# A recurrence over pairs of tokens: scans of half the length, with the decay folded into k and r

## The chip, the cores and the metric

The kernel runs on one core of one Trainium2 chip. The metric is the device time of one execution in microseconds. The kernel before takes 1902.09 us (median of 3 runs, 1901.77 to 1902.61). In what follows PE is the matmul engine (PEld its weight loads), DVE the vector engine, ACT the scalar engine, POOL the general engine (GpSimd) and SP the engine that issues most DMAs.

## The reference

The input is 32 batches of 128 rows (channels) by 512. Two layers follow one another in each batch. The first is a cross attention between x and a context: both are normalised over their 512 columns, projected with 128x128 weights (Mn, Mm), multiplied to 512x512 scores, put through a softmax, and applied to a third projection; the input is added. The second layer is an RWKV block over 128 tokens of 512 features, with the context's first rows as its state. Its heart is a recurrence in 32 heads of 16x16 states:

```
xm = xa[:, :, None] + sx[:, :, None] * (maa_stack + xxx)        # five mixes of token t and t-1
w = exp(-exp(time_decay + tanh(xw @ td_w1) @ td_w2));  r, k, v = projections of their mixes
def step(s, rkvw):
    a = k_t[..., :, None] * v_t[..., None, :]
    out = einsum('bhi,bhij->bhj', r_t, u * a + s)
    s = a + w_t[..., :, None] * s
    return (s, out)
x1 = x + groupnorm(out) * silu(xg @ Wg.T) @ Wo.T
out = x1 + sigmoid(xr2 @ Wfr.T) * (square(relu(xk2 @ Wfk.T)) @ Wfv.T)
```

All of it is in fp32.

## The kernel before

A batch is one unit of work, and the kernel is a software pipeline written out by hand. There are 36 steps; in step s each engine works on batch s (`b0`), s-1 (`b1`), s-2 (`b2`), s-3 (`b3`) and s-4 (`b4`). Names beginning with `att_` are the attention, `mid_` the mixes and projections, `wkv_` the recurrence, `tail_` the group norm up to the channel mix, `fin_` the end. Each engine has a function `step` which lists, in its fixed order, the jobs of one step. Every engine runs its list strictly in that order and waits on semaphores for the others; `Steps` turns a label and a batch number into a semaphore count. PSUM banks 0 to 3 are a ring for the front jobs and banks 6 and 7 a ring for the back jobs (`FRONT_JOBS`, `BACK_JOBS`): a job waits until the job that used its bank last has been read (`bank_free`). Bank 4 holds the sums of the recurrence, bank 5 its transposed output.

The recurrence lies with one partition for each (head, i) pair in chunks of 128 of the 512 features, and is cut into eight units `u`: chunk `u % 4` and eight of the 16 columns j. For a unit, SP loads `vrep`, v repeated over the 16 partitions of a head, from a copy of v in DRAM (`load_vrep`, 512 KB, two buffers). DVE multiplies it by k into `S` (`wkv_outer`, L606, 8 x 127 columns), POOL writes the start state into column 0 of each of the eight rows (`wkv_s0`, L446), DVE runs the scan over 1024 columns with the decay `wrep` (`wkv_scan`, L615; the decay's column 0 is 0, so each row starts anew), and multiplies the states by r in place (`wkv_read`, L624). PE then sums over i (`wkv_sum`, L1129) and the buffer is free again. ACT fills `wrep` by an exponential that repeats each chunk eight times (`decay`, L863). The term with u is added apart: `rku` = r k on POOL (`wkv_rk`, L436), a matmul per chunk (`tail_C`, L1138), and `bonus` = v times that on DVE (`tail_o`, L637).

The other names that matter: `att_O` (L1049) is the attention's last matmul; `att_xin` (L531) adds the residual, `att_xst` and `att_xag` (L536, L542) take its statistics, POOL makes the inverse deviation by an addition and a power (`rstd_of`, L400 and L402), `att_rstd1` (L502) makes the bias `nm1`, ACT normalises into `xhat` (L779), and PE transposes it (`mid_Tx`). The residual `xin` has two buffers and is copied by a DMA to `xres` (`copy_xres`, L330), from which `tail_x1` (L659) reads it two steps later. `tail_var`, `tail_hrs` and `tail_gn` are the group norm.

## Time and profile before

| | |
|---|---|
| median of the runs | 1902.09 us |
| profiled execution | 1903.22 us |
| its span, first to last instruction | 1901.3 us |
| busy PE / PEld / DVE / ACT / POOL | 93 / 65 / 93 / 63 / 66% |
| scan L615, 256 instructions | 602.6 us |
| read L624 and outer product L606 | 343.3 and 341.0 us |
| DMA | 189.32 MB, mean 100 GB/s |

Busy time is the time in which an engine executed something; PE's weight loads overlap its matmuls and stand apart. An engine at 93% over the span can still be idle only at the two ends, where the pipeline fills and drains. The table's sums are those of one execution.

### The profile page before, as it was taken

Reading aid. Unit: us, or ns where it says so; the run is one execution under the profiler, and the core shown is the slowest. Engines: PE = TensorE matmul, PEld = TensorE weight load, DVE = VectorE, ACT = ScalarE, POOL = GpSimd, SP = SyncE. Lnnn points to the kernel's source line nnn. Section 1 sums busy time; section 2 is a strip of 40 time slices with the busy share of each in tenths; the row PEclk is TensorE's granted clock in tenths of the full one; section 3 lists DMA queues with packets and bytes.
Section 4 is the critical chain, followed back from the end, with each engine's and each line's share of the span. In section 5 each row is a group of like instructions: output and inputs, shape, how many; then the busy total and the mean of one; then the engine's idle time right before and its main releaser. Section 6 shows DMA issues by size and latency. Waiting matters only on the chain.

```text
span 1901.3 us, 34866 instructions
## 1 busy us (share of the span) xinstructions
PE 1761.4 (93%) x12356; PEld 1228.6 (65%) x12356; DVE 1775.5 (93%) x2084; ACT 1196.1 (63%) x2849; POOL 1253.3 (66%) x822
## 2 busy tenths in 40 slices
...
GB/s 239 60 98 96 106 102 92 101 104 102 100 106 99 92 101 104 104 101 102 99 91 102 106 106 98 103 98 91 105 107 103 98 103 96 95 107 96 91 66 11
DMA packets 86203, 189.32 MB, mean 100 GB/s; under 512 B 18800, under 2 KB 35312, under 8 KB 85008
## 3 DMA queue, kind: packets, MB, share of 16 engines
...
q8 instruction: 100, 1.64, 0.4%
q14 instruction: 71, 0.58, 0.1%
...
## 4 chain that ended last, share of the span: by engine, by line
DVE 52%; issue 24%; POOL 11%; PE 7%; ACT 6%; DVEq 0%; DMA 0%; POOLq 0%; ACTq 0%; SPq 0%
DVE S L615 18%; DVE S L606 8%; DVE S L624 8%; POOL rstd L402 7%; ACT wrep L863 3%; DVE xf L578 3%; PE bank L1004 3%; DVE nmax L521 3%; DVE xx L568 2%; PE bank L1011 1%; DVE xin L531 1%; POOL rstd L400 1%; DVE st L663 1%; DVE x L659 1%; POOL S L446 1%
## 5 line engine op out<-in xcount | busy, mean ns | idle before, releaser
L615 DVE TENSOR_TENSOR_SCAN S<-wrep,S 128x1024 f32<-128x1024 f32 x256 | 602.6, 2354 | 2.1 <-ACT wrep L863 0.8
L446 POOL COPY S<-s 128x8 f32<-128x8 f32 x256 | 281.4, 1100 | 291.9 <-PE bank L1129 283.3
L624 DVE TENSOR_TENSOR S<-S,rT 128x1024 f32<-128x1024 f32 x256 | 343.3, 1341 | 2.8 <-ACT rT L868 1.6
L606 DVE TENSOR_TENSOR S<-vrep,kT 128x1016 f32<-128x1016 f32 x256 | 341.0, 1332 | 0.0
L430 POOL TENSOR_TENSOR xf<-xf,xa 128x512 f32<-128x512 f32 x160 | 249.3, 1558 | 89.8 <-DVE xf L578 87.5
L402 POOL TENSOR_TENSOR rstd<-rstd,mhalf 128x1 f32<-128x1 f32 (+1 forms) x96 | 211.3, 2201 | 8.0
L1129 PE MATMUL bank<-S,slide 128*32 128x256 f32 x2048 | 165.0, 394 | 23.8 <-DVE S L624 23.7
L827 ACT ACTIVATE bank<-bank,par 128x128 f32<-128x128 f32 x640 | 175.8, 366 | 10.6 <-PE bank L1085 10.6
L402 POOL TENSOR_TENSOR hrs<-hrs,mhalf 128x32 f32<-128x32 f32 x32 | 174.8, 5462 | 2.7
L400 POOL TENSOR_SCALAR rstd<-mv 128x1 f32<-128x1 f32 (+1 forms) x96 | 36.2, 377 | 204.9 <-DVE mv L542 151.8
L790 ACT ACTIVATE prob<-bank,nmax 128x512 f32<-128x512 f32 x128 | 88.3, 690 | 102.4 <-DVE nmax L521 101.5
L1036 PE MATMUL bank<-probT 128*128 128x512 f32 x256 | 133.7, 606 | 2.0 <-ACT prob L790 1.2
L1011 PE MATMUL bank<-Wo,ogT 128*128 128x512 f32 x256 | 123.8, 630 | 10.2 <-DVE ogT L653 10.2
L1004 PEld LDWEIGHTS bank<-xf,Wk 128*128 128x128 f32 x1024 | 116.8, 192 | 22.7 <-POOL xf L430 21.6
L863 ACT ACTIVATE wrep<-ez 128x1016 f32<-128x1016 f32 x128 | 130.0, 1041 | 0.0
L1004 PE MATMUL bank<-xf,Wk 128*128 128x128 f32 x1024 | 122.0, 278 | 8.6 <-DVE xf L578 8.5
L1004 PE MATMUL bank<-xf,Wv 128*128 128x128 f32 x1024 | 125.5, 283 | 3.9
L907 ACT ACTIVATE xp<-bank,prev 128x128 f32<-128x128 f32 x256 | 129.0, 504 | 0.0
L1004 PE MATMUL bank<-xk,Wfk 128*128 128x128 f32 x1024 | 124.2, 282 | 4.4 <-DVE xk L678 4.4
L1004 PEld LDWEIGHTS bank<-xf,Wr 128*128 128x128 f32 x1024 | 118.8, 195 | 13.3 <-issue 13.2
L1004 PEld LDWEIGHTS bank<-xf,Wv 128*128 128x128 f32 x1024 | 120.3, 197 | 9.1 <-POOL xf L430 8.6
L1004 PEld LDWEIGHTS bank<-xf,Wg 128*128 128x128 f32 x1024 | 116.7, 192 | 13.9 <-POOL xf L430 13.5
...
## 6 DMA issues: line engine op xcount, KB each, us to landing
vrep<-v_dram SPq DMA_DIRECT2D x256, 512.0 KB
xc<-x_c SPq DMA_DIRECT2D x32, 256.0 KB, 6.4
xs<-x_s SPq DMA_DIRECT2D x32, 256.0 KB, 7.1
v_dram<-vT ACTq DMA_DIRECT2D x32, 256.0 KB, 2.3
xres<-xin SPq DMA_DIRECT2D x32, 256.0 KB, 6.1
out<-rr ACTq DMA_DIRECT2D x32, 256.0 KB, 2.0
...
```

The source lines that it names most:

```text
L402: po.tensor_tensor(rs, rs, mhalf[:, 0:rs.shape[1]], ALU.pow).then_inc(own.sem, 1)
L430: po.tensor_tensor(xf[:, b, :, :], xf[:, b, :, :], xa[:, :, 1:P + 1], ALU.add).then_inc(pool_mid.sem, 1)
L446: po.tensor_copy(S[:, u % 2, :, 0], s0[:, p, k:k + UJ]).then_inc(pool_wkv.sem, 1)
L606: ve_.tensor_tensor(S[:, u % 2, :, 1:P], vrep[:, u % 2, :, 0:P - 1], k, ALU.mult).then_inc(dve_wkv.sem, 1)
L615: ve_.tensor_tensor_scan(s, wrep[:, u % C, :, :].rearrange("p j t -> p (j t)"), s, 0.0, ALU.mult, ALU.add).then_inc(dve_wkv.sem, 1)
L624: ve_.tensor_tensor(s, s, rT[:, p, u % C, :].unsqueeze(1).broadcast_to([P, UJ, P]), ALU.mult).then_inc(dve_wkv.sem, 1)
L827: last = sc.activation(ps, ps, ACT.Identity, bias=col("maa_stack", c, MIX.index(f)))
L863: sc.activation(wrep[:, c, :, 1:P], ez[:, c, 0:P - 1].unsqueeze(1).broadcast_to([P, UJ, P - 1]), ACT.Exp, scale=-1.0).then_inc(act_decay.s ...
L1004: last = pe.matmul(ps[:, o * P:(o + 1) * P], w[:, c, o * P:(o + 1) * P], src[:, c, :], start=(c == 0), stop=(c == C - 1))
L1011: last = pe.matmul(bank_of(job)[:, :], src[:, c, :], w[:, c, :], start=(c == 0), stop=(c == C - 1))
L1036: pe.matmul(bank_of(f"S{t}")[:, :], Mn[:, t * P:(t + 1) * P], Mm, start=True, stop=True).then_inc(pe_att.sem, 1)
L1129: last = pe.matmul(bank[SUM_BANK][32 * g:32 * g + 32, 2 * P * half:2 * P * (half + 1)], ones, S[:, u % 2, g:UJ:4, :], start=(c == 0), stop ...
```

## The change

The recurrence advances two tokens at a time. With tokens 2m and 2m+1 as pair m, the state before pair m+1 is w(2m) w(2m+1) S + w(2m+1) k(2m) v(2m) + k(2m+1) v(2m+1). So k of the first token of a pair is multiplied by the second's decay, r of the second token by the first's decay, and the scan has 64 columns in each row in place of 128. What token 2m+1 receives from token 2m of its own pair is r(2m+1) k(2m) v(2m) summed over a head, the pair coefficient: one matmul more, and two vector instructions.

- DVE per batch: eight scans of 512 columns in place of 1024; `wkv_outer` writes 8 x 126 columns to a new tile `A`; eight new `wkv_pair` add the two tokens of each pair into `S` (8 x 63 columns); `wkv_read` reads each state twice and writes 1024 columns to `A`; new `mid_kw`, `mid_rw`, `tail_o2` and `tail_ob` of 256 columns each.
- ACT: `mid_k` and `mid_r` make a second, strided half copy; `mid_w` takes the exponential once; `decay` only repeats it, over 504 columns.
- POOL: new `mid_ez2` and `wkv_rk2`, products of 256 columns; `wkv_s0` waits for the reading product in place of PE's sum.
- PE: new `tail_C2`, one matmul of 256 columns; `wkv_sum` reads `A`.
- `xin` has three buffers; `xres` and its copy go.
- The order of the jobs is new on all five engines and in both rings. Among others `att_O` of a batch is now the first job of the following PE step, `tail_FK` and `tail_C` follow it, and `att_xag` and `att_rstd1` stand at the start of the following DVE step.

```diff
+T2 = P // 2
-    "Tx:1 Mn:0 V:0 Mm:0 W1:1 S0:0 Wt:1 S1:0 S2:0 Mv:1 Mw:1 S3:0 Mk:1 Mr:1 Mg:1 Vp:1 D1:1 Kp:1 "
-    "T0:0 T1:0 T2:0 T3:0 O:0 D2:1 E2:1 Rp:1 G:1").split())]
+    "O:1 V:0 Tx:1 W1:1 Mn:0 Wt:1 Mm:0 Mv:1 Mw:1 S0:0 S1:0 S2:0 Vp:1 Mk:1 Mr:1 Mg:1 D1:1 S3:0 Kp:1 "
+    "D2:1 E2:1 Rp:1 T0:0 T1:0 T2:0 G:1 T3:0").split())]
-    "FR:4 FV:4 Tg:3 Wo:3 Tx2:3 FK:3 C:2").split())]
+    "FK:4 C:3 C2:3 FR:4 FV:4 Tg:3 Wo:3 Tx2:3").split())]
...
-        xin = sb("xin", [P, 2, E])
+        xin = sb("xin", [P, 3, E])
...
# POOL
+                po.tensor_tensor(ez2[:, :, :], first(ez[:, :, :]), second(ez[:, :, :]), ALU.mult).then_inc(pool_ez2.sem, 1)
+                po.tensor_tensor(rk2[:, :, :], second(rT[:, :, :]), first(kT[:, :, :]), ALU.mult).then_inc(pool_rk2.sem, 1)
-                v1 = held(eng, regs[1], pe_wkv.count(f"r{(u - 2) % U}", n if u >= 2 else n - 1))
+                v1 = held(eng, regs[1], dve_read.count(f"q{(u - 2) % U}", n if u >= 2 else n - 1))
# DVE
-                eng.wait_ge(xres_copied[p], 16 * m)
+                eng.wait_ge(dve_tail.sem, dve_tail.count("x1", n - 3))
+                ve_.tensor_tensor(first(kt[:, p, :, :]), first(kT[:, :, :]), second(ez[:, :, :]),
+                                  ALU.mult).then_inc(dve_pre.sem, 1)
+                ve_.tensor_tensor(second(rt[:, p, :, :]), second(rT[:, :, :]), first(ez[:, :, :]),
+                                  ALU.mult).then_inc(dve_pre.sem, 1)
-                ve_.tensor_tensor(S[:, u % 2, :, 1:P], vrep[:, u % 2, :, 0:P - 1], k, ALU.mult).then_inc(dve_wkv.sem, 1)
+                ve_.tensor_tensor(A[:, u % 2, :, 0:P - 2], vrep[:, u % 2, :, 0:P - 2], k, ALU.mult).then_inc(dve_outer.sem, 1)
+            def wkv_pair(n, m, p, u):
+                eng.wait_ge(dve_outer.sem, dve_outer.count(f"a{u}", n))
+                a = A[:, u % 2, :, 0:P - 2]
+                ve_.tensor_tensor(S[:, u % 2, :, 1:T2], first(a), second(a), ALU.add).then_inc(dve_pair.sem, 1)
-                ve_.tensor_tensor(s, s, rT[:, p, u % C, :].unsqueeze(1).broadcast_to([P, UJ, P]),
-                                  ALU.mult).then_inc(dve_wkv.sem, 1)
+                out4 = A[:, u % 2, :, :].rearrange("p j (m k) -> p j m k", k=2)
+                s = S[:, u % 2, :, :].unsqueeze(3).broadcast_to([P, UJ, T2, 2])
+                r = rt[:, p, u % C, :].rearrange("p (m k) -> p m k", k=2).unsqueeze(1).broadcast_to([P, UJ, T2, 2])
+                ve_.tensor_tensor(out4, s, r, ALU.mult).then_inc(dve_read.sem, 1)
...
# DVE, start and end of the new step
+                if b2: wkv_outer(*b2, 1)
+                if b1: att_xag(*b1)
+                if b2: mid_gate(*b2)
+                if b4: tail_mix(*b4, 1)
+                if b1: att_rstd1(*b1)
...
+                if b2: wkv_outer(*b2, 6)
+                if b2: wkv_pair(*b2, 6)
                 if b3: tail_rstd(*b3)
+                if b2: wkv_outer(*b2, 7)
                 if b2: wkv_scan(*b2, 6)
+                if b2: wkv_pair(*b2, 7)
+                if b1: mid_kw(*b1)
                 if b2: wkv_read(*b2, 6)
+                if b2: wkv_scan(*b2, 7)
+                if b1: mid_s0c(*b1)
+                if b1: wkv_outer(*b1, 0)
+                if b2: wkv_read(*b2, 7)
+                if b1: wkv_pair(*b1, 0)
+                if b3: tail_mix(*b3, 0)
                 if b0: att_xin(*b0)
+                if b1: mid_rw(*b1)
                 if b0: att_xst(*b0)
# ACT
+                sc.activation(ez[:, :, :], ez[:, :, :], ACT.Exp, scale=-1.0).then_inc(act_mid.sem, 1)
-                sc.activation(wrep[:, c, :, 1:P], ez[:, c, 0:P - 1].unsqueeze(1).broadcast_to([P, UJ, P - 1]),
-                              ACT.Exp, scale=-1.0).then_inc(act_decay.sem, 1)
+                sc.activation(wrep[:, c, :, 1:T2], ez2[:, c, 0:T2 - 1].unsqueeze(1).broadcast_to([P, UJ, T2 - 1]),
+                              ACT.Copy).then_inc(act_decay.sem, 1)
# PE, and the start of its new step
+                pe.matmul(bank_of("C2")[:, 0:C * T2], head_rep[:, :], rk2[:, :, :].rearrange("p c m -> p (c m)"),
+                          start=True, stop=True).then_inc(pe_tail.sem, 1)
+                if b1: att_O(*b1)
+                if b3: wkv_sum(*b3, 7)
+                if b4: tail_FK(*b4)
+                if b3: tail_C(*b3)
+                if b0: att_V(*b0)
+                if b3: tail_C2(*b3)
                 if b1: mid_Tx(*b1)
+                if b4: fin_FR(*b4)
```

## Rows read from the trace of the kernel before

**Rows 1.** The page, busy time of each engine over the whole span.
```profile
PE 1761.4 (93%) x12356; PEld 1228.6 (65%) x12356; DVE 1775.5 (93%) x2084; ACT 1196.1 (63%) x2849; POOL 1253.3 (66%) x822
```

**Rows 2.** Windows, busy us (instructions) of each engine, granted clock, DMA share, 27 periods.
```profile
171.00:1673.28 1502.28, 1452.54 (x10424) 1017.85 (x10423) 1488.33 (x1756) 1006.23 (x2403) 1077.60 (x674) 1.00 0.38 101
```

**Rows 3.** Chain of waits in order of time: start, us, what.
```profile
171.00 2.68 POOL rstd L402
...
1617.70 2.69 POOL rstd L402
```

**Rows 4.** Timeline of DVE in one step: start, us, engine, line, op, tiles.
```profile
1003.88 1.20 DVE L606 TENSOR_TENSOR S<-vrep,kT 128x1016 f32<-128x1016 f32 x1
1005.00 0.16 DVE L669 BATCH_NORM_AGGREGATE mv<-st 128x2 f32<-128x6 f32 x1
1005.10 0.65 DVE L578 TENSOR_TENSOR xf<-bank,sx 128x512 f32<-128x512 f32 x1
1005.67 2.27 DVE L615 TENSOR_TENSOR_SCAN S<-wrep,S 128x1024 f32<-128x1024 f32 x1
...
1015.23 0.74 DVE L531 SCALAR_TENSOR_TENSOR xin<-bank,bo,xc 128x512 f32<-128x512 f32 x1
1016.00 0.69 DVE L536 BATCH_NORM_STATS2 st<-xin 128x6 f32<-128x512 f32 x1
...
1048.49 2.28 DVE L606 TENSOR_TENSOR S<-vrep,kT 128x1016 f32<-128x1016 f32 x1
```

**Rows 5.** Timeline of PE in the same step.
```profile
1014.22 0.37 PE L1115 MATMUL bank<-dt,tw 64*128 64x128 f32 x1
...
1019.60 3.74 PE L1004 MATMUL bank<-xk,Wfk 128*128 128x128 f32 x32
1023.17 1.06 PE L1138 MATMUL bank<-rku,head_u 128*128 128x128 f32 x8
1024.16 0.64 PE L1129 MATMUL bank<-S,slide 128*32 128x256 f32 x8
...
1029.28 0.60 PE L1016 MATMUL bank<-ident,xhat 128*128 128x128 f32 x4
...
1039.10 1.02 PE L1023 MATMUL bank<-prob,attw 128*128 128x512 f32 x2
1039.96 1.25 PE L1064 MATMUL bank<-w,xx 128*128 128x160 f32 x8
```

**Rows 6.** Groups by line and shape: busy us, mean ns, idle before.
```profile
L863 ACT ACTIVATE wrep<-ez 128x1016 f32<-128x1016 f32 x128 | 130.0, 1041 | 0.0
...
L402 POOL TENSOR_TENSOR hrs<-hrs,mhalf 128x32 f32<-128x32 f32 x32 | 174.8, 5462 | 2.7
...
L400 POOL TENSOR_SCALAR hrs<-hvar 128x32 f32<-128x32 f32 x32 | 66.7, 2086 | 21.9 <-DVE hvar L642 21.7
L436 POOL TENSOR_TENSOR rku<-rT,kT 128x512 f32<-128x512 f32 x32 | 66.6, 2082 | 0.0
```

**Rows 7.** DMA issues: tiles, queue, count, KB each, median us to landing.
```profile
v_dram<-vT ACTq DMA_DIRECT2D x32, 256.0 KB, 2.3
...
st<-state SPq DMA_DIRECT2D x64, 2.0 KB, 6.0
```

**Rows 8.** Timeline of SP in the same step.
```profile
1005.16 0.59 SPq L320 DMA_DIRECT2D vrep<-v_dram  x1
1005.84 0.42 SPq L297 DMA_DIRECT2D st<-state  x1
```

**Rows 9.** Timeline of ACT in the same step.
```profile
1022.18 0.81 ACT L779 ACTIVATE xhat<-xin,nmr,rstd 128x512 f32<-128x512 f32 x1 [3.26 <-DVE nmr L502]
```

**Rows 10.** Timeline of POOL in the same step.
```profile
1005.64 2.68 POOL L402 TENSOR_TENSOR rstd<-rstd,mhalf 128x1 f32<-128x1 f32 x1
...
1018.06 0.50 POOL L400 TENSOR_SCALAR rstd<-mv 128x1 f32<-128x1 f32 x1 [3.84 <-DVE mv L542]
```

**Rows 11.** Timeline of POOL while the pipeline fills.
```profile
76.41 0.56 POOL L402 TENSOR_TENSOR rstd<-rstd,mhalf 128x1 f32<-128x1 f32 x1
```

More of the change, by code:

```diff
@@ L146, in build @@
         ez = sb("ez", [P, C, P])
[L147 to L150 removed]
+        kT = sb("kT", [P, C, P])
+        rT = sb("rT", [P, C, P])
+        kt = sb("kt", [P, 2, C, P])
+        rt = sb("rt", [P, 2, C, P])
+        ez2 = sb("ez2", [P, C, T2])
+        wrep = sb("wrep", [P, C, UJ, T2])
         vT = sb("vT", [P, 2, C, P])
@@ L157, in build @@
         vrep = sb("vrep", [P, 2, UJ, P])
-        S = sb("S", [P, 2, UJ, P])
+        A = sb("A", [P, 2, UJ, P])
+        S = sb("S", [P, 2, UJ, T2])
+        rk2 = sb("rk2", [P, C, T2])
+        pv = sb("pv", [P, C, T2])
         st0 = sb("st0", [P, 2, C])
@@ L179, in by_chunk, with first, second @@
             return ap.rearrange("p (c t) -> p c t", c=C)
+        def first(ap):
+            return ap.rearrange("p c (m k) -> p c m k", k=2)[:, :, :, 0]
+        def second(ap):
+            return ap.rearrange("p c (m k) -> p c m k", k=2)[:, :, :, 1]
         xn = prob[:, 0, :]
@@ L198, in build @@
         vrep_loaded = [sem(f"vrep_loaded{i}") for i in range(2)]
-        xres_copied = [sem(f"xres_copied{i}") for i in range(2)]
         v_stored = sem("v_stored")
@@ L210, in units @@
             return " ".join(f"{x}{u}" for u in range(U) for x in text.split())
-        dve_att = Steps(sem("dve_att"), "stats aggr nm mx0 mx1 ri0 mx2 ri1 mx3 ri2 ri3 xin xst xag nm1")
-        dve_mid = Steps(sem("dve_mid"), "sx xx mv mw mk mr mg s0m s0c g")
-        dve_wkv = Steps(sem("dve_wkv"), units("a s q"))
-        dve_tail = Steps(sem("dve_tail"), "o1 var o3 og x1 st ag nm xk2 xr2")
+        dve_att = Steps(sem("dve_att"), "stats aggr nm mx0 mx1 mx2 ri1 ri0 mx3 ri2 ri3 xin xst xag nm1")
+        dve_mid = Steps(sem("dve_mid"), "sx xx s0m mv mw mk mr mg s0c g")
+        dve_pre = Steps(sem("dve_pre"), "kw rw")
+        dve_outer = Steps(sem("dve_outer"), units("a"))
+        dve_pair = Steps(sem("dve_pair"), units("b"))
+        dve_scan = Steps(sem("dve_scan"), units("s"))
+        dve_read = Steps(sem("dve_read"), units("q"))
+        dve_tail = Steps(sem("dve_tail"), "o1 o2 ob var o3 og x1 st ag nm xk2 xr2")
         dve_fin = Steps(sem("dve_fin"), "y")
-        act_att = Steps(sem("act_att"), "xn yn Mn Mm v p0 p1 n0 p2 p3 n1 n2 n3 T0 T1 T2 T3 xhat")
-        act_mid = Steps(sem("act_mid"), "xa tn tx dt vT k ez r th")
-        act_mix = Steps(sem("act_mix"), "bw bv bk br bg")
+        act_att = Steps(sem("act_att"), "v xn yn Mn Mm p1 p2 p0 n0 n1 p3 n2 n3 T0 T1 T2 T3 xhat")
+        act_mid = Steps(sem("act_mid"), "xa tn tx vT dt ez k dw r th")
+        act_mix = Steps(sem("act_mix"), "bv bw bk br bg")
         act_decay = Steps(sem("act_decay"), "w0 w1 w2 w3")
@@ L322, in load_vrep @@
                     .then_inc(vrep_loaded[u % 2], 16)
-            def copy_xres(n, m, p):
-                v0 = held(sp, regs[0], dve_att.count("xin", n))
-                v1 = held(sp, regs[1], dve_tail.count("x1", n - 2))
-                sp.wait_ge(setup_loaded[0], 32)
-                sp.wait_ge(dve_att.sem, v0)
-                sp.wait_ge(dve_tail.sem, v1)
-                sp.dma_start(xres[:, p, :], xin[:, p, :]).then_inc(xres_copied[p], 16)
             load_x(0, 0)
```

323 lines of the change are left out of this document (174 added, 149 removed).

## The prediction

> **What bounds the kernel now.** I read the page's busy shares first [rows 1]: PE and DVE both stand at 93%, POOL at 66%, ACT at 63%, so two engines are candidates. The window over 27 periods tells them apart [rows 2]: divided by 27, DVE is busy for 55.12 us, PE for 53.80, POOL for 39.9 and ACT for 37.3 of a period of 55.64. The reader is to see 0.5 us of idle DVE and 1.8 us of idle PE in each step, at a granted clock of 1.00 (the 2.4 GHz level). The period is the distance of equal pieces of the chain: (1617.70 - 171.00) / 26 = 55.64 us [rows 3]. So DVE sets the step, and PE stands 1.8 us behind it; no saving on DVE can bring more than the distance to PE unless PE's work shrinks, and the change adds to PE's. Outside 31 periods there are 1901.3 - 31 x 55.64 = 176 us of filling and draining.
>
> **DVE: the scan.** A 1024-column scan takes 2.27 us when undisturbed [rows 4]. The aggregate of six numbers takes 0.16 us, so some 0.15 us is fixed, and 512 columns come to 2.12 / 2 + 0.15 = 1.21 us. Eight per batch: 8 x 1.06 = 8.5 us saved.
>
> **DVE: what is added.** Eight pair additions of 504 elements. The nearest row is the 512-element tensor_tensor of 0.65 us, behind whose start the next instruction starts 0.57 us later [rows 4], since DVE's instructions overlap by about 0.08 us. I take 0.58 us. No row shows an operand read at every second element, nor one read twice (in the reading product). From above the scan bounds both, since it takes twice as long for a column as the 1016-element outer product (1.20 us) does: 1.13 us for a pair, 2.2 us in place of 1.12 us for a reading product. From below stands contiguous speed. I take that end, which is the nearer row, an addition or product of two tensors: 8 x 0.58 = 4.7 us. The products kw and rw and the sums o2 and ob have 256 elements: 0.15 + 0.50 / 2 - 0.08 = 0.33 us each, 1.3 us together (bounds 0.15 and 0.58 each). The outer product (1008 in place of 1016) and the reading product (1024) keep their durations. Net: -8.5 + 4.7 + 1.3 = -2.5 us, so DVE goes from 55.1 to 52.6 us of work a step.
>
> The Trainium skill, SBUF — State Buffer, section Specifications (TRN2), says that two accesses within a 16-byte line are needed for full bandwidth; every second fp32 element still gives two, so by that rule the pairs run at 0.58 us, and the sum stays; were the penalty paid all the same, it would be the strided rival below. No row of before shows it.
>
> **PE.** The sums over S become sums over A, of the same shape. tail_C2 adds one matmul of 256 columns. Mn, of 512 columns, occupies 1039.96 - 1039.10 = 0.86 us [rows 5], so C2 costs 0.43 us (0.2 to 0.9). PE's own work: 53.8 + 0.4 = 54.2 us a step. The new order moves PE's jobs past one another, but each stays whole, so their sum stays.
>
> **ACT and POOL.** ACT repeats 504 in place of 1016 columns (1.041 us [rows 6], now about 0.6: -1.7 us a step), and gains one exponential of 512 (0.6) and two strided half copies from PSUM (0.4 each, bounds 0.2 and 0.6): nothing net, beside 37 of 55 us busy. POOL gains two products of 256, each about half of rku's 2.08 us [rows 6] (0.6 to 2.15): 39.9 to 42 us, not a bound. It writes the first column of S after the reading product rather than after PE's sum, so PE's part of that wait goes, and DVE's order is what is late next. POOL can still be late with hrs: 2.09 + 5.46 us [rows 6] between tail_var and tail_gn, and rk2 (1.0) is now ahead of it on POOL. DVE has scan1, outer2, s0, read1, pair2, two maxima, scan2, mix0 and read2 in between, 8.1 us, against 8.6 on POOL, of which the first 2.09 is mostly waiting beside a scan (its minimum work is some 0.3): hidden with little margin. Lost cover costs up to 0.5 us of DVE, or 1.5 if s0(2) is late as well, and DVE has 1.6 to spare under PE.
>
> **DMA.** The xres copy goes from SP's queue (256 KB per batch), and att_xin now waits for x1 of three batches ago, long past. On SP vrep, st0, st1, s0 and x are moved past one another; x and the states are wanted over 10 us after their issue. A vrep load is issued when outer(u-2) is done. Tightest is outer 0 of the next batch: pair6, outer7, scan6, pair7, kw, read6, scan7 and s0c lie between it and outer6, 6.2 us. A 2 KB state load lands 6.0 us after its issue in the median [rows 7], where it is issued 0.68 us behind a vrep load in the same queue [rows 8]; so vrep has landed by 6.7 us, and no earlier than the 2.3 us of v_dram's 256 KB [rows 7]. Cost 0 to 0.5 us of DVE a step, which its slack takes up; I take none.
>
> **The order.** O(n) now opens PE's step, one step later than before, and att_xin stands near the end of DVE's; behind it rw, xst, outer1, xag, two POOL instructions, nm1, xhat on ACT, and PE's Tx. Behind O, PE has sum7, FK, C, V and C2 until Tx: 0.57 + 3.57 + 0.99 + 0.99 + 0.43 = 6.55 us [rows 5] (V as C, the sum's 0.64 less its overlap of 0.07). The chain, undisturbed: xin 0.70, rw 0.33, xst 0.61, outer1 1.12, xag 0.18 [rows 4], POOL 0.3 + about 1.2 beside the gate and the mix, nm1 0.16, xhat 0.81, and 0.3 for handovers: 5.7 us. It fits by 0.8 us. Behind Tx's wait stand all later PE jobs, so whatever this chain is late is lost once a step. Walking the other handovers in the same manner (scores to maxima, mixes to POOL to Vp, Kp and Rp, oT to Wo, Wo to x1, sum6 and the copy of T3 to the next O) I find each within 0 to 1 us of its partner, none clearly late. I put 0.5 us a step (0 to 1.4) for what such narrow handovers leave idle on PE; today it is 1.8, with DVE the slower engine.
>
> **Sum.** Period 54.2 + 0.5 = 54.7 us; 31 x (55.64 - 54.7) = 29 us. In the drain DVE works through the last units alone: 8 x 0.5 = 4 us less, about 1 more for C2, o2 and ob: -3 (-8 to +8, the fill's new order included). The profiled execution took 1903.2 us for its span of 1901.3: 1903.2 - 32 = 1871; it stood 1.1 us over the median of the runs, so 1870.
>
> **Rivals.**
> PE fed without a gap. For it, DVE has 1.6 us of slack under PE; against it, PE is at 97% today with its longest wait at a handover from ACT, not DVE. Period 54.2: 1902 - 31 x 1.44 - 3 = 1854. Chance 0.12.
>
> The chain from O to Tx is late (the slower side). For it: today the same chain takes from O's end at 1014.2 [rows 5] to xhat's end at 1022.99 [rows 9], 8.8 us, and Tx starts only at 1029.28, with 6.3 us to spare; the change leaves 6.55 us in all. With disturbed rows, outer 2.28 [rows 4], the POOL steps 0.50 and 2.68 [rows 10], and xin 0.74, rw 0.41, xst 0.69, xag 0.18, nm1 0.16, xhat 0.81, it is 8.45 us, 1.9 over the cover: period 56.1, 1902 + 31 x 0.46 - 3 = 1913. It decides from 8.0 us on, where PE's 54.2 plus the stall reach 55.64. Against it: today's 8.8 us hold a mix, a sum, a scan and a read of other batches; and the power takes 0.56 us when DVE leaves it alone [rows 11], 2.68 beside a 2.27 us scan, and no DVE instruction of that stretch is now above 1.2 us. Chance 0.13.
>
> Rows 4, 10 and 11 show that: 2.68 - 0.56 is about a scan. The Trainium skill, SBUF — State Buffer, section Terms, calls the port of DVE and GpSimd exclusive and held for the whole instruction, and the trace agrees; by that rule the power takes at most 0.56 + 1.21 = 1.8 us there, and the chain stays at about 6.5 us.
>
> Strided operands at half speed: DVE 52.6 + 8 x 0.55 = 57.0 us, 1902 + 31 x 1.36 - 3 = 1941. Nothing in the rows is for it, and nothing excludes it. Chance 0.06.
>
> The gain is eaten by small waits, in ACT's in-order queue above all (fifteen instructions between nm1 and the tanh that Wt waits for): period 55.6, 1902. Chance 0.07.
>
> **The numbers.** The forecast (periods 54.3 to 55.4, so 1857 to 1891) has 0.62. Faster by over 0.2%, about what a measurement of this kernel can tell from no change: 0.62 + 0.12 = 0.74; within it 0.07; slower 0.13 + 0.06 = 0.19. The range, 1853 to 1909, leaves out the strided case, most of the late chain, and a part of the gapless one.
>
> **What would show it.** Scans at 1.2 us, pairs at 0.66, reading products still at 1.22, DVE's work 52 to 53 us a step; PE busy for 54.2 us of a 54.7 us period, above DVE's share; Tx without a wait of over 0.5 us on xhat. I am wrong if DVE is still the fuller engine, if pairs take over 0.9 us, or if PE waits over 1.4 us a step in all.

## The result, and the profile after

| | before | after |
|---|---|---|
| median of the runs, us | 1901.93 (1901.75 to 1902.61, 4 runs) | 1890.38 (1889.85 to 1892.81, 4 runs) |
| profiled execution, time / span, us | 1903.2 / 1901.3 | 1890.35 / 1888.5 |
| `xin` of batches 0, 1, 2 starts, us | 34.29, 74.17, 125.95 | 35.58, 83.39, 136.75 |
| first y (batch 0) on DVE, us | 205.06 | 215.11 |
| y of batch 27, us | 1707.72 | 1697.92 |
| period over these 27 steps, us | 55.654 | 54.919 |
| from there to the end, us | 193.6 | 190.6 |

The ratio is 0.9942 (95% interval 0.9928 to 0.9956): the change makes the kernel 11.5 us faster. Forecast were 32. The last four lines, read from DVE's timeline (`xin` is att_xin, y is fin_y), say where: the fill is 10.0 us longer, 27 periods bring 27 x 0.735 = 19.8 us, the rest 3.0; 19.8 + 3.0 - 10.0 = 12.8 is the difference of the spans. The forecast had 25.4 for the 27 periods and 6.8 for everything outside them.

The page after, busy time of each engine over the span, to be held against [rows 1]:

```profile
PE 1785.4 (95%) x12420; PEld 1235.2 (65%) x12420; DVE 1743.5 (92%) x2468; ACT 1174.2 (62%) x2945; POOL 1048.8 (56%) x886
```

Windows after, columns as in [rows 2]: 25 periods, and one step that was not held up:

```profile
178.10:1551.33 1373.23, 1365.55 (x9700) 949.94 (x9701) 1355.60 (x1926) 913.92 (x2301) 825.11 (x675) 1.00 0.37 97
1002.69:1057.47 54.78, 54.54 (x389) 37.99 (x389) 54.17 (x78) 36.52 (x93) 33.16 (x27) 1.00 0.36 97
```

The order of the engines has turned: PE is busy for 54.54 of 54.78 us, DVE for 54.17. PE was forecast at 54.2, DVE at 52.6, POOL at 42. So PE is a little fuller than worked out, DVE much fuller, and POOL, at 33, freer: with 825.11 / 25 = 33.0 us it does less than before in spite of two added products.

The groups of DVE by line and shape in 200 to 1600 us (count | busy us, mean ns of one | idle before):

```profile
L657 DVE TENSOR_TENSOR_SCAN S<-wrep,S 128x512 f32<-128x512 f32 x205 | 284.5, 1388 | 0.0
L669 DVE TENSOR_TENSOR A<-S,rt 128x1024 f32<-128x1024 f32 x204 | 263.3, 1291 | 0.0
L642 DVE TENSOR_TENSOR A<-vrep,kt 128x1008 f32<-128x1008 f32 x203 | 243.0, 1198 | 3.5 <-DMA vrep<-v_dram 2.8
L648 DVE TENSOR_TENSOR S<-A 128x504 f32<-128x504 f32 x204 | 187.7, 930 | 0.9
```

The scan's mean went from 2346 ns (the same view before) to 1388, so eight save 7.7 us, not 8.5. The pairs take 930 ns in the mean and not 660. Less the 0.08 us by which DVE's instructions overlap, which the forecast took off too, eight cost 6.8 us, not 4.7.

What makes a pair of 0.67 us take 0.93 in the mean is seen by laying DVE beside POOL. Timelines after, DVE and then POOL, of the same 10 us:

```profile
1043.21 2.34 DVE L648 TENSOR_TENSOR S<-A 128x504 f32<-128x504 f32 x2
...
1049.06 2.20 DVE L657 TENSOR_TENSOR_SCAN S<-wrep,S 128x512 f32<-128x512 f32 x1
```

```profile
1042.12 2.30 POOL L480 TENSOR_TENSOR rr<-rr,x 128x512 f32<-128x512 f32 x1
...
1048.09 2.09 POOL L438 TENSOR_TENSOR xf<-xf,xa 128x512 f32<-128x512 f32 x1 [3.67 <-DVE xf L600]
```

POOL's sum runs to 1044.42. The first pair starts at 1043.21 and can't move until then: 1.21 us of waiting, and twice 0.57 of work, make the 2.34. In the same way the scan at 1049.06 stands until POOL's sum ends at 1050.18, and then takes 1.1 us. Not every POOL instruction does this. In the same step, POOL's power of 32 columns and a pair inside it:

```profile
1031.52 6.36 POOL L410 TENSOR_TENSOR hrs<-hrs,mhalf 128x32 f32<-128x32 f32 x1
```

```profile
1033.73 0.68 DVE L648 TENSOR_TENSOR S<-A 128x504 f32<-128x504 f32 x1
```

This pair, and a scan of 1.21 us that starts at 1035.06, run at full speed while the power is going on.

POOL's own groups over the whole span have become shorter where DVE's instructions have:

```profile
L410 POOL TENSOR_TENSOR hrs<-hrs,mhalf 128x32 f32<-128x32 f32 x32 | 200.5, 6266 | 2.7
...
L450 POOL TENSOR_TENSOR rku<-rT,kT 128x512 f32<-128x512 f32 x32 | 41.0, 1281 | 22.9 <-PE bank L1222 22.8
```

rku went from 2082 ns [rows 6] to 1281; the power of 32 columns went the other way, 5462 to 6266.

The chain that the first rival was about, PE's timeline after in one step:

```profile
1013.47 3.70 PE L1133 MATMUL bank<-probT,v_att 128*128 128x512 f32 x8
1017.10 0.64 PE L1213 MATMUL bank<-A,slide 128*32 128x256 f32 x8
...
1023.13 0.60 PE L1230 MATMUL bank<-rk,head_rep 128*128 128x256 f32 x2
1023.57 0.60 PE L1100 MATMUL bank<-ident,xhat 128*128 128x128 f32 x4
```

O gives way to sum7 at 1017.10, and sum7, FK, C, V and C2 run behind it without a gap; Tx at 1023.57 shows no wait for xhat. The cover of 6.5 us is there, and the chain fits in it.

The periods one by one are 54.78, 54.78, 55.99, 54.97, 54.79, 54.78, 54.78, 55.61, 54.77, 54.93, ...: 19 of 27 stand within 0.06 of 54.78, and eight are longer by 0.15 to 1.2. Before, all but the last stood within 0.02 of 55.65. Two views say what five of the eight are. The waits in 200 to 1700 us (us in total, times, longest), and two steps of the chain of waits:

```profile
DVE nmr L524 <- POOL rstd L410: 12.7, 27, 0.5
PE bank L1088 <- ACT prob L857: 4.5, 27, 0.2
DVE A L642 <- DMA vrep<-v_dram: 2.8, 5, 1.2
```

```profile
347.00 7.78 DMA vrep<-v_dram
...
624.23 10.53 DMA vrep<-v_dram
```

The first two waits come once in each step and are small. The third comes five times, up to 1.2 us, each in one of the longer periods: the wait of 1.18 us stands in the period that is 1.21 longer. On the chain of waits a vrep load of 7.0 to 10.5 us stands before four of the five. The other three longer periods (by 0.15 to 0.2) show no wait for vrep. The 256 KB of v_dram also land in 7.3 us now, in place of 2.3 [rows 7]:

```profile
v_dram<-vT ACTq DMA_DIRECT2D x32, 256.0 KB, 7.3
```

The fill, while batch 1 enters. PE and DVE after:

```profile
70.57 3.84 PE L1088 MATMUL bank<-xf,Wr 128*128 128x128 f32 x32
74.38 1.53 PE L1100 MATMUL bank<-ident,prob 128*128 128x128 f32 x12
75.75 3.74 PE L1088 MATMUL bank<-xf,Wg 128*128 128x128 f32 x32
...
79.76 3.60 PE L1133 MATMUL bank<-probT,v_att 128*128 128x512 f32 x8
```

```profile
66.54 0.69 DVE L600 TENSOR_TENSOR xf<-bank,sx 128x512 f32<-128x512 f32 x1 [0.51 <-ACT bank L894]
67.15 0.68 DVE L543 TENSOR_REDUCE nmax<-bank 128x1 f32<-128x512 f32 x1
...
83.39 0.75 DVE L553 SCALAR_TENSOR_TENSOR xin<-bank,bo,xc 128x512 f32<-128x512 f32 x1 [7.28 <-PE bank L1133]
```

and before:

```profile
68.79 1.91 PE L1016 MATMUL bank<-ident,prob 128*128 128x128 f32 x16
70.54 3.60 PE L1049 MATMUL bank<-probT,v_att 128*128 128x512 f32 x8
...
74.71 3.84 PE L1004 MATMUL bank<-xf,Wr 128*128 128x128 f32 x32
78.39 3.78 PE L1004 MATMUL bank<-xf,Wg 128*128 128x128 f32 x32
```

```profile
56.70 0.68 DVE L521 TENSOR_REDUCE nmax<-bank 128x1 f32<-128x512 f32 x1
```

Counted from the start of xin of batch 0, O of batch 1 starts at 36.3 us before and at 44.2 after. Two things hold it: the last maximum of its scores stands behind the last mix on DVE, 10 us later than before (67.15, 56.70), and G of batch 0, 3.6 us, stands ahead of T3 and O. By the same count T starts 38.8 us after xin of batch 0 and not 34.5, which is 4.3 of the 7.9 us; G is the rest. In the full pipeline both are hidden; in the fill nothing else is there to hide them. DVE's idle time in front of xin, 7.28 us, was no shorter before (8.16): it is the whole chain that has moved.

### The profile page after: what moved, and what is told of

It is laid out like the page before. It is cut to its first block, busy times and chain, and to the rows that moved or that the text cites. A ratio compares the mean times of both kernels' runs of the same rounds, so it can differ in the third digit from the quotient of the medians.

```text
span 1888.5 us, 35795 instructions
## 1 busy us (share of the span) xinstructions
PE 1785.4 (95%) x12420; PEld 1235.2 (65%) x12420; DVE 1743.5 (92%) x2468; ACT 1174.2 (62%) x2945; POOL 1048.8 (56%) x886
## 4 chain that ended last, share of the span: by engine, by line
PE 49%; DVE 27%; issue 17%; DMA 3%; POOL 2%; ACT 1%; ACTq 0%; DVEq 0%; POOLq 0%; SPq 0%
PE bank L1088 17%; PE bank L1095 6%; DVE A L642 5%; PE bank L1133 5%; DVE S L657 5%; PE bank L1100 4%; DVE A L669 4%; PE bank L1213 3%; PE bank L1107 3%; DVE nmax L543 3%; DVE xf L600 3%; DMA vrep<-v_dram 3%; PE bank L1120 2%; DVE S L648 2%; PE bank L1169 2%
## 5 line engine op out<-in xcount | busy, mean ns | idle before, releaser
L466 POOL COPY S<-s 128x8 f32<-128x8 f32 x256 | 197.6, 773 | 321.9 <-DVE A L669 212.2
L657 DVE TENSOR_TENSOR_SCAN S<-wrep,S 128x512 f32<-128x512 f32 x256 | 354.5, 1385 | 0.7 <-ACT wrep L941 0.6
L669 DVE TENSOR_TENSOR A<-S,rt 128x1024 f32<-128x1024 f32 x256 | 330.9, 1293 | 0.1
L642 DVE TENSOR_TENSOR A<-vrep,kt 128x1008 f32<-128x1008 f32 x256 | 309.6, 1210 | 10.2 <-DMA vrep<-v_dram 4.8
L648 DVE TENSOR_TENSOR S<-A 128x504 f32<-128x504 f32 x256 | 230.4, 910 | 1.2
L408 POOL TENSOR_SCALAR rstd<-mv 128x1 f32<-128x1 f32 (+1 forms) x96 | 71.7, 747 | 243.9 <-DVE mv L564 143.5
L1213 PE MATMUL bank<-A,slide 128*32 128x256 f32 x2048 | 166.2, 397 | 14.4 <-DVE A L669 14.4
L1088 PEld LDWEIGHTS bank<-xk,Wfk 128*128 128x128 f32 x1024 | 121.4, 198 | 19.1 <-DVE xk L733 19.1
L1088 PE MATMUL bank<-xf,Wr 128*128 128x128 f32 x1024 | 122.0, 277 | 5.1 <-ACT prob L857 5.1
L869 ACT ACTIVATE probT<-bank 128x512 f32<-128x512 f32 x128 | 72.4, 594 | 86.9 <-PE bank L1100 84.4
```

What stands on the lines that cost most here:

```text
L466: po.tensor_copy(S[:, u % 2, :, 0], s0[:, p, k:k + UJ]).then_inc(pool_wkv.sem, 1)
L642: ve_.tensor_tensor(A[:, u % 2, :, 0:P - 2], vrep[:, u % 2, :, 0:P - 2], k, ALU.mult).then_inc(dve_outer.sem, 1)
L648: ve_.tensor_tensor(S[:, u % 2, :, 1:T2], first(a), second(a), ALU.add).then_inc(dve_pair.sem, 1)
L657: ve_.tensor_tensor_scan(s, wrep[:, u % C, :, :].rearrange("p j t -> p (j t)"), s, 0.0, ALU.mult, ALU.add).then_inc(dve_scan.sem, 1)
L669: ve_.tensor_tensor(out4, s, r, ALU.mult).then_inc(dve_read.sem, 1)
L1088: last = pe.matmul(ps[:, o * P:(o + 1) * P], w[:, c, o * P:(o + 1) * P], src[:, c, :], start=(c == 0), stop=(c == C - 1))
```

## Experiments

All have the kernel after as their base. Times are medians beside runs of the kernel before on the same chip, ratios are against it. "Period" is the mean of the 27 as above, "typical" the value that most of them have.

| kernel | us | ratio (95%) | period / typical | first y minus xin of batch 0 |
|---|---|---|---|---|
| after | 1890.38 | 0.9942 (0.9928 to 0.9956) | 54.92 / 54.78 | 179.5 |
| pe_plus | 1932.35 | 1.0164 (1.0145 to 1.0183) | 56.27 / 56.17 | 181.1 |
| pe_minus | 1883.61 | 0.9903 (0.9888 to 0.9918) | 54.71 / 54.60 | 179.2 |
| dve_plus | 1932.56 | 1.0163 (1.0148 to 1.0178) | 56.11 / 55.92 | 182.0 |
| dve_minus | 1888.48 | 0.9923 (0.9908 to 0.9938) | 54.82 / 54.79 | 182.0 |
| pool_light | 1891.17 | 0.9939 (0.9925 to 0.9954) | 54.87 / 54.78 | 180.8 |
| pair_contig | 1893.04 (one run) | | 54.92 / 54.79 | 179.3 |
| vrep3 | 1887.88 | 0.9925 (0.9912 to 0.9937) | 54.79 / 54.79 | 180.8 |
| vrep3_again | 1885.47 | 0.9902 (0.9885 to 0.9918) | 54.78 / 54.79 | 180.8 |
| fill_order | 1897.93 | 0.9988 (0.9977 to 0.9999) | 54.97 / 54.79 | 186.2 |
| fill_vrep3 | 1895.60 | 0.9967 (0.9956 to 0.9979) | 54.79 / 54.79 | 188.5 |
| g_last_vrep3 | 2026.03 | 1.0647 (1.0632 to 1.0661) | 59.5 / 59.6 | 183.5 |
| g_first_vrep3 | 1921.01 | 1.0093 (1.0078 to 1.0108) | 56.11 / 56.11 | 179.4 |
| fill_g_vrep3 | 1884.47 | 0.9923 (0.9908 to 0.9937) | 54.79 / 54.79 | 180.0 |

Before, the last column is 170.8. All kernels down to vrep3_again have the fill order of the kernel after, and the column still goes from 179.2 to 182.0, the latter also in dve_minus, which only leaves work out: less than 2 us in it can't be told from no change.

**Which engine sets the period: one edit to each side of PE and of DVE.**

```diff
# pe_plus: one more matmul of 512 columns in FR, overwritten by FR's own
+                pe.matmul(bank_of("FR")[:, :], xr2[:, 0, :], W["Wfr"][:, 0, :], start=True, stop=True)
# pe_minus: FR without its fourth chunk
-                proj_N("FR", W["Wfr"], xr2).then_inc(pe_fin.sem, 1)
+                proj_N("FR", W["Wfr"], xr2, C - 1).then_inc(pe_fin.sem, 1)
# dve_plus: x1's statistics three times
+                ve_.bn_stats(st63[:, :], x1[:, :])
+                ve_.bn_stats(st64[:, :], x1[:, :])
# dve_minus: the gate and both tail mixes on the first of four chunks
-                ve_.scalar_tensor_tensor(gT[:, p, :, :], gT[:, p, :, :], 1.0, by_chunk(bank_of("G")[:, :]),
+                ve_.scalar_tensor_tensor(gT[:, p, 0, :], gT[:, p, 0, :], 1.0, bank_of("G")[:, 0:P],
...
-                ve_.tensor_tensor(dst[:, :, :], dst[:, :, :], xp2[:, i, :, 0:P], ALU.add).then_inc(dve_tail.sem, 1)
+                ve_.tensor_tensor(dst[:, 0, :], dst[:, 0, :], xp2[:, i, 0, 0:P], ALU.add).then_inc(dve_tail.sem, 1)
```

> The changed kernel with one more matmul of 512 columns in PE's job FR of every batch (0.86 us of PE work, output unchanged). Theory A, PE sets the changed kernel's period (54.54 us busy of 54.78): period 54.78 + 0.86 = 55.6, time 1890 + 31 x 0.86 = 1917. Theory B, DVE sets it (54.17 us busy, the rest handovers) and PE's work hides beside it: at most 0.24 us is hidden, 1890 + 31 x 0.6 = 1909.

> The changed kernel with one matmul of 512 columns less in FR (the fourth chunk of the sigmoid's projection is left out), 0.86 us of PE work a step less. Theory A: the period falls until DVE's 54.17 us of work stop it, to 54.3 to 54.4: 1890 - 31 x 0.45 = 1876. Theory B: DVE sets the period already, no change, 1890 (within 3).

> The changed kernel with two more statistics of 512 columns on DVE in every batch, behind tail_st (1.2 us of DVE work, output unchanged). DVE goes from 54.17 to 55.4 us of work. Theory A: 0.6 us of it fits beside PE, period about 55.5, 1890 + 31 x 0.7 = 1912. Theory B: the whole 1.2 us shows, 1890 + 37 = 1927.

> The changed kernel with DVE's gate product and both tail_mix additions made for one chunk of 128 columns in place of four (three quarters of that work left out, 1.2 us of DVE a step). Theory A, PE sets the period: no change, 1890 (within 4; a few us may come from the ends). Theory B, DVE sets it: down to PE's 54.54, 1890 - 31 x 0.24 = 1883 or less.

Windows 200 to 1600 us of pe_minus and of dve_minus (columns as in [rows 2]), one fence each:

```profile
200.00:1600.00 1400.00, 1382.11 (x9861) 960.45 (x9863) 1384.72 (x1969) 931.18 (x2352) 846.72 (x691) 1.00 0.36 97
```

```profile
200.00:1600.00 1400.00, 1393.43 (x9884) 967.74 (x9886) 1365.95 (x1967) 934.76 (x2354) 837.62 (x689) 1.00 0.37 97
```

With 1.2 us of work a step taken from DVE (its busy time in this window falls by 16.3 us, 0.6 a step) the typical period does not move (54.79): PE sets it. With 0.86 us taken from PE it falls by 0.18 only, under half of what was expected, and DVE is then busy for 1384.72 of 1400 us, 99%: DVE is the next bound, right behind. The waits of pe_minus have DVE's wait for POOL's rstd (11.8 us in 25 steps, 0.47 each), and DVE's 54.1 us of work with it make the 54.6. In the other direction PE's added work costs more than itself and DVE's nearly all of itself: 0.86 us on PE cost 1.39, 1.2 us on DVE 1.14. All expectations for the added work were too low: pe_plus, 1932, lies 15 us above theory A and 23 above theory B; dve_plus, 1933, lies 20 us above theory A, by which half of DVE's work hides, and 6 above theory B, by which none does. So the two removals say which engine comes first, and the two additions that neither has room. The waits of pe_plus in 200 to 1600 us say what the additional 0.5 us are:

```profile
DVE hvar L698 <- ACT sq L966: 21.9, 25, 0.9
PE bank L1095 <- DVE ogT L709: 16.7, 25, 0.7
...
DVE A L642 <- PE bank L1213: 9.7, 25, 0.4
```

The matmul stands ahead of To, so DVE's var waits 0.9 us for sq; all of DVE behind it moves back, and PE then waits 0.7 for ogT. None of the three stands among the waits of PE's matmuls and of DVE in the steady part of the kernel after. In dve_plus PE waits 0.7 us a step for a reading product. With both engines above 98% here, a delay put into one comes back from the other.

**What stretches the pairs: stride or POOL.**

```diff
# pool_light: POOL's last residual sum (L480) on 8 of 512 columns
-                po.tensor_tensor(rr[:, :], rr[:, :], x1[:, :], ALU.add).then_inc(pool_fin.sem, 1)
+                po.tensor_tensor(rr[:, 0:8], rr[:, 0:8], x1[:, 0:8], ALU.add).then_inc(pool_fin.sem, 1)
# pair_contig: the same sizes, contiguous operands
-                ve_.tensor_tensor(S[:, u % 2, :, 1:T2], first(a), second(a), ALU.add).then_inc(dve_pair.sem, 1)
+                ve_.tensor_tensor(S[:, u % 2, :, 1:T2], a[:, :, 0:T2 - 1], a[:, :, T2 - 1:P - 2], ALU.add).then_inc(dve_pair.sem, 1)
```

> The changed kernel with POOL's last addition of the residual made for 8 of 512 columns (the rest is left out), which takes 2.2 us of POOL work from beside pairs 3 and 4. Theory P, the pairs take 0.91 us in the mean in place of 0.66 because POOL's instructions hold them, not because of their stride: mean at or under 0.80 us, DVE's work down by about 1 us a step, and the time unchanged within 4 us, since PE sets the period. Rival, the stride costs: mean still 0.9 us.

> The kernel after, with the pair additions reading the two contiguous halves of A in place of every second element (wrong partners, same sizes, same waits, same place). Theory S (operands with a stride of two elements slow DVE): the shortest pair falls from 0.650 us towards 0.58 or less and the mean from 0.91. Theory P (the pairs are held by POOL's spans beside them): shortest, median and mean stay within 0.02 us of 0.650, 0.682 and 0.91. The time stays at 1888 to 1892 in both, since PE sets the period.

The pairs' group in 200 to 1600 us, in pool_light and then in pair_contig:

```profile
L648 DVE TENSOR_TENSOR S<-A 128x504 f32<-128x504 f32 x204 | 159.9, 793 | 0.8
```

```profile
L648 DVE TENSOR_TENSOR S<-A 128x504 f32<-128x504 f32 x204 | 187.7, 930 | 0.9
```

With contiguous operands the mean is what it was, 930 ns (187.7 us both times), and the shortest pair takes 667 ns where the strided one takes 668: the stride of two elements costs nothing. Without one POOL instruction out of 27 in a step it falls by 137 ns, 8 x 0.137 = 1.1 us a step. So POOL holds pairs: this one instruction accounts for over half of the 2.1 us by which eight exceed 0.67 each; for the rest no POOL instruction was taken away. The time did not move (1891.17, typical period 54.78), and where the 1.1 us went is in the waits of pool_light, a wait of DVE that the kernel after does not have:

```profile
DVE xf L600 <- ACT bank L894: 27.4, 26, 1.1
```

DVE arrives 1.1 us earlier at a mix and waits for it there. So the step of the forecast that undersized the pairs cost DVE slack, but no time of its own.

**The longer periods: a third vrep buffer.**

```diff
-        vrep = sb("vrep", [P, 2, UJ, P])
+        vrep = sb("vrep", [P, 3, UJ, P])
-        dt = sb("dt", [P, P])
+        dt = txn[:, 0:P]
...
+                g = n * U + u
-                sp.dma_start(vrep[:, u % 2, :, :].rearrange("p j t -> p (j t)"),
+                sp.dma_start(vrep[:, g % 3, :, :].rearrange("p j t -> p (j t)"),
```

> The changed kernel with three vrep buffers in place of two, so a load is issued one unit earlier (dt shares a buffer with txn for the room). Theory V, the longer periods among the 54.78 us ones (mean 54.92) come from vrep loads that land after outer is ready, because the new order leaves 6.2 us for one: no wait of outer on vrep, mean period 54.79, 1890 - 4 = 1886. Rival: the load itself is slow now and then whatever its issue, or PE has the slack: 1889 to 1891.

> The kernel with three vrep buffers once more, beside g_first_vrep3 on the same chip. Both theories: period 54.79, first y 215 to 218, 1886 to 1889, ratio to before 0.9925 within 0.0013.

Outer products in 200 to 1600 us in vrep3:

```profile
L644 DVE TENSOR_TENSOR A<-vrep,kt 128x1008 f32<-128x1008 f32 x203 | 242.8, 1197 | 0.3
```

The idle time before them fell from 3.5 to 0.3 us, no wait for vrep is left, and all 27 periods stand between 54.77 and 54.80. That is 27 x 0.13 = 3.6 us, and the theory is borne out for the period. The profiled runs show less of it at their ends (1889.10 and 1889.51) than the medians do (1887.88 and 1885.47): in the profiled run of vrep3 the first y comes at 217.49, 2.4 us later than in the kernel after, so 1.2 of the 3.6 us are left. The fill is not the same in every run; the six times of vrep3 go from 1881.4 to 1889.3, and that the fill makes this spread is likely, but only profiled runs show it.

**The fill: four orders of its jobs.**

```diff
# fill_order, at steps 1 and 2 only (PE; ACT and DVE in the same sense)
+                if s == 1:
+                    for c in range(C):
+                        att_T(*b0, c)
+                    att_O(*b0)
                 if b1: mid_P(*b1, "r", "Rp", "Wr")
...
+                if s == 2: att_V(*b0)
# DVE
+                if s == 2: mid_rw(*b2)
+                if s == 2: mid_gate(*b2)
# fill_vrep3: fill_order and vrep3
# g_last_vrep3: vrep3, the PSUM ring as in g_first_vrep3 below, and in every step
-                if b1: att_O(*b1)
                 if b3: wkv_sum(*b3, 7)
...
-                if b1: mid_P(*b1, "g", "G", "Wg")
                 if b0: att_T(*b0, 3)
                 if b3: tail_Tx2(*b3)
                 if b2: wkv_sum(*b2, 6)
+                if b0: att_O(*b0)
+                if b1: mid_P(*b1, "g", "G", "Wg")
# g_first_vrep3: vrep3, T3 and O ahead of G at step 1 only, but the PSUM ring changed for all steps
-    "O:1 V:0 Tx:1 W1:1 Mn:0 Wt:1 Mm:0 Mv:1 Mw:1 S0:0 S1:0 S2:0 Vp:1 Mk:1 Mr:1 Mg:1 D1:1 S3:0 Kp:1 "
-    "D2:1 E2:1 Rp:1 T0:0 T1:0 T2:0 G:1 T3:0").split())]
+    "V:0 Tx:1 W1:1 Mn:0 Wt:1 Mm:0 Mv:1 Mw:1 S0:0 S1:0 S2:0 Vp:1 Mk:1 Mr:1 Mg:1 D1:1 S3:0 Kp:1 "
+    "D2:1 E2:1 Rp:1 T0:0 T1:0 T2:0 T3:0 O:0 G:1").split())]
# fill_g_vrep3: vrep3 with its own ring, and
+                if s == 1:
+                    att_T(*b0, 3)
+                    att_O(*b0)
                 if b1: mid_P(*b1, "g", "G", "Wg")
-                if b0: att_T(*b0, 3)
+                if b0 and s != 1: att_T(*b0, 3)
```

> The changed kernel with another order in its second and third step alone: in step 1 PE makes T0 to T3 and O of batch 1 ahead of Rp and G of batch 0, ACT makes the decay and xhat ahead of r, and DVE leaves rw and the gate of batch 0 to step 2. Theory F, the 10 us of later filling (first fin_y at 215.1 us, 205.1 in the kernel before) come from O(1) standing behind Rp and G (7.3 us of PE work): xin of batch 1 falls from 83.4 to about 76 us, the first fin_y to 208, the time to 1883. Rival: PE has the same work to do sooner or later, and what is gained at step 1 is waited for at step 2: 1889 to 1891.

> Both: the order of steps 1 and 2 and the three vrep buffers. If both theories hold and the two add: 1890 - 7 - 4 = 1879. If only one holds, 1883 or 1886.

In fill_order O of batch 1 ran ahead of Rp and G, and the fill became 7 us longer, not shorter. PE there:

```profile
71.97 3.68 PE L1107 MATMUL bank<-ident,prob 128*128 128x128 f32 x16 [3.74 <-ACT prob L865]
...
85.62 3.81 PE L1095 MATMUL bank<-xf,Wg 128*128 128x128 f32 x32 [2.14 <-ACT rt L953]
```

T waits 3.74 us for the scaled scores: the late maximum, which Rp had covered. Counted from xin(0), xin(1) came only 1.1 us earlier (46.7 us in place of 47.8). Then G waited 2.14 us for rt, an outer product waited 5.38 us for PE's sum (2.46 in the kernel after), and xin(2) came 6.6 us later. Both theories missed it, at 1883 and at 1889 to 1891 against 1897.93; fill_vrep3, at 1895.60, lies above all three of its values for the same reason, its period being vrep3's.

> Three vrep buffers as in vrep3, and on PE the job G of the older batch (3.5 us, 16 matmuls) moves, in every step, from ahead of T3 and O to behind O; the DVE, ACT and POOL orders stay. Nothing is left out. In the first steps O of batch 1 then has only Rp, and not Rp and G, ahead of it that was not there in the kernel before. Theory F2 (the fill costs what PE work was put ahead of O of batch 1, and the steady period is PE's busy time plus 0.25 us): xin of batch 1 comes 3.5 us earlier than in vrep3 (80.1 in place of 83.65), the first y 3 to 4 us earlier (about 214 in place of 217.5), the period stays 54.79, and the time is 1884.5 (1883 to 1886). Theory L (the fill is set by the whole chain of handovers of the first batches, of which any one takes the place of the one removed, as it was when the first two steps were put in another order): the first y moves by under 1.5 us, the period stays, 1887 to 1889. Theory G (G late holds th, the gate and W1's bank in every step): period 54.9 to 55.4, 1892 to 1907.

> vrep3 with one thing moved, in the fill alone: at the step in which batch 1 enters, T3 and O of batch 1 stand on PE ahead of G of batch 0 (3.5 us), and V of batch 2 no longer waits for that G's reader; the PE order of all other steps and the DVE, ACT and POOL orders stay. Nothing is left out. Theory F2 (the fill costs the PE work put ahead of O of batch 1): xin of batch 1 at 80.1 (83.65 in vrep3), xin of batch 2 and the first y 3 to 4 us earlier (first y near 214), the period 54.79, the time 3.5 us under vrep3's. Theory L (whatever handover is next sets the first y): xin of batch 1 at 80.1 all the same, the first y earlier by under 1.5 us, the time within 1.5 us of vrep3's.

g_last_vrep3 is the warning of the series: in each step one job of 3.5 us moved past T3, Tx2 and sum6, O came ahead of sum7, and three jobs changed their place in the PSUM ring. The period goes from 54.79 to 59.5, which none of its three theories had (55.4 at most). Its waits in 200 to 1600 us:

```profile
PE bank L1215 <- DVE A L671: 68.5, 23, 3.0
DVE A L644 <- PE bank L1215: 58.0, 23, 2.6
```

sum6 now stands there 3 us before its reading product is done; sum7 comes only behind O and G, 7.3 us of PE work, and the outer product that needs its buffer waits 2.6 us for it. Two engines wait for each other in a ring. In g_first_vrep3 the steady order was left alone and only the ring changed; its two theories both had the period at 54.79, and it came to 56.11. The same view:

```profile
DVE A L644 <- PE bank L1215: 29.0, 25, 1.2
PE bank L1090 <- ACT probT L871: 27.3, 25, 1.1
```

G got the bank of T1 and waits 1.1 us in each step for ACT to copy T1 out of it, which costs 1.33 us a step. That wait is not among those of g_last_vrep3, where G comes later; what the ring alone adds to its 4.7 us was not tried.

> vrep3 with only the order in which PE issues three jobs changed, at the one step in which batch 1 enters: T3 and O of batch 1 ahead of G of batch 0. PSUM banks and every other step as in vrep3, so that the 1.1 us per step that G waited for its new bank in g_first_vrep3 is not there. Nothing is left out. Theory F2 (the fill costs the PE work put ahead of O of batch 1): xin of batch 1 at 78 to 80 (83.9 in vrep3), first y 213.5 to 214.5 (217.7), period 54.79, the time 3 to 4 us under vrep3: 1882 to 1884. Theory L (the next handover takes it back; here V waits for G's reader, 2 us, behind which Tx of batch 1 stands): first y 216 to 218, time within 1.5 us of vrep3's 1885.5 to 1887.9. If the period grows by 0.1 or more, the cost of the job order in the steady steps is not only the bank.

Here the period stayed at 54.79, and G alone was moved, in one step. PE:

```profile
72.29 2.21 PE L1102 MATMUL bank<-ident,prob 128*128 128x128 f32 x16
74.81 3.67 PE L1135 MATMUL bank<-probT,v_att 128*128 128x512 f32 x8 [0.31 <-ACT probT L871]
78.31 3.73 PE L1090 MATMUL bank<-xf,Wg 128*128 128x128 f32 x32
```

xin(1) came at 78.52, and the first y at 213.24, 4.3 us before vrep3's 217.49. At first sight that is theory F2. It is not: xin(0), which the edit does not touch, came at 33.24 in place of 36.66. From xin(0) on, xin(1) is 1.7 us earlier (45.3, 47.0), and the first y 0.8 (180.0, 180.8), which is within the spread. In g_first_vrep3, where T3 does not wait for a bank, xin(1) is 3.5 us earlier (43.5) and the first y 1.4 (179.4). In both, over half of what was gained at O was given back by the next handovers, as theory L has it, and the time of fill_g_vrep3, 1884.47, cannot be told from vrep3's 1885.47 and 1887.88.

What moved xin(0) is seen first in the same six matmuls of batch 0's scores, behind the same wait, in vrep3 and in fill_g_vrep3, each followed by the window of just these six:

```profile
16.51 4.77 PE L1122 MATMUL bank<-probT 128*128 128x512 f32 x6 [0.78 <-ACT probT L855]
...
16.51:21.28 4.77, 4.76 (x6) 1.85 (x6) 1.38 (x2) 0.23 (x1) 0.00 (x0) 1.00 1.02 429
```

```profile
16.56 2.84 PE L1122 MATMUL bank<-probT 128*128 128x512 f32 x6 [0.78 <-ACT probT L855]
...
16.56:19.40 2.84, 2.84 (x6) 1.05 (x6) 1.38 (x2) 0.09 (x1) 0.00 (x0) 1.00 1.00 418
```

The six take 4.77 and 2.84 us, 1.9 of the 3.4 us between the two xin(0). The granted clock reads 1.00 in both stretches, so the profile does not show what slowed them. The next two matmuls of the scores take 1.86 us at a granted clock of 0.56, and 1.10 us at 1.00; there the clock is the difference, full speed being the level of 2.4 GHz and half of it that of 1.2. O of batch 0, later in the fill, takes 4.77 us at 0.77 and 3.98 us at 0.92. Kernels whose first 37 us are the same have their xin(0) at 33.2 to 36.9 us, so the fill must be read from its first landmark on.

## Why the prediction was wrong

The direction and the mechanism were right: DVE was relieved, PE became the bound, at a typical period of 54.78 us where 54.7 was forecast. The size was wrong by 20 us, and two terms hold it.

**The ends: the step that failed.** The step "-3 (-8 to +8, the fill's new order included)" put the new order into the bounds and not into the sum. Outside the 27 periods the forecast gives -3 and four more periods' gain, -6.8 in all; measured is +10.0 - 3.0 = +7.0. That is 13.8 of the missing 19.3 us of span: 10.0 the fill, 3.8 the drain, whose last four steps brought 3.0 in place of 6.8. Of the fill's +10.0, 1.3 lie ahead of xin(0) and vary by run; 7.9 arise up to xin(1), with the late maximum and G ahead of O (the trace; fill_order and fill_g_vrep3 show each of them holding O); the rest is within the spread. The prediction had walked O's new place for the steady chain, and the new list of jobs says that O stands behind Rp and G: 7 us for whoever has nothing else to do. None of the orders tried had it back at the first y: moving G gave 0.8 to 1.4 us, within the spread, and moving Rp and G with what depends on them cost 6.7. An order of the fill that is as short as before's was not found, and stays open. So does the drain's 3.8: DVE waits there for vrep three times (0.5 to 0.8 us), but vrep3, without these waits, takes the same 190.6 us from the y of batch 27 to the end.

**The period.** 0.735 us a step in place of 0.94. Of the 0.2 missing, 0.13 are the waits for vrep, shown by vrep3: the prediction bounded their cost by 0 to 0.5 of DVE and took none, on the ground that a load has landed by 6.7 us and DVE's slack takes up the rest. The loads on the chain took 7.0 to 10.5 us, and the slack was not there: of DVE's 0.6 us of idle time a step, 0.47 is its wait for POOL's rstd (11.8 us in 25 steps), and the waits for vrep lengthened their periods by their whole length. The other 0.08 is the typical step, where PE's 54.54 and 0.24 of idle stand for 54.2 + 0.5. C2 itself takes 0.44 until the next job starts, as forecast; where PE's other 0.3 comes from was not tried.

**DVE.** The pairs were the term that was mis-sized: 6.8 us in place of 4.7, and their mean of 0.93 us is past the 0.9 that the prediction had named as a sign of being wrong. The stride, which held the wide bound, is free, as pair_contig shows; what was left out is POOL, by pool_light for over half of it. The same rows [rows 10, 4] that show POOL's power held up by a scan had to be read the other way round too. The Trainium skill, SBUF — State Buffer, section Terms, says of the pair of ports that "the loser **fully blocks**", and the pair of 1.21 + 2 x 0.57 us beside POOL's sum agrees. Beside POOL's power of 32 columns the trace does not: a pair of 0.68 and a scan of 1.21 us run inside its 6.36 us, so the port is not held against DVE for the whole of that instruction. The prediction had used the rule only for how long POOL waits for DVE. The scans saved 7.7 where 8.5 stood, the outer products got 1.1 shorter and the reading products 0.3 where nothing stood, and the four of 256 columns are right (0.41, 0.41, 0.40 and 0.42 us, less 0.08 each). DVE at 54.2 in place of 52.6 did not set the typical period (dve_minus, pool_light), but it took the slack on which the entries at no cost had rested.

**The rivals.** The late chain from O to Tx did not come: the power takes 1.14 us there, in the bounds given by a port held for one short instruction. Strided operands: no. A gapless PE: close, 0.24 us idle, but above a larger sum. Small waits: ACT's queue shows none above 0.2 us on PE. The measured time does lie in the stated range, but that is owed to the range's width, which took in no change at all as well.
